# First rows asked for ahead of an expert's weights, in a kernel of two graph layers and two expert layers

## The reference, cut to what matters

```python
gate_scores = x @ Wg + bg                       # 8 experts
_, idx = jax.lax.top_k(gate_scores, K)          # K = 2 of them for each row
mask = jax.nn.one_hot(idx, E, dtype=x.dtype).sum(axis=-2)
h = jax.nn.gelu(jnp.einsum('td,edh->teh', xf, W1) + b1[None], approximate=False)
y = jnp.einsum('teh,ehd->ted', h, W2) + b2[None]
out = jnp.einsum('ted,te->td', y, mf)           # x = x + out
```

## Time and profile before

| what | value |
|---|---|
| median of 3 runs | 1220.38 us (1215.12 to 1221.03) |
| the profiled execution's own time | 1220.32 us |
| span in the profile | 1218.5 us |
| outside the span | 1.8 us |
| mean granted TensorE clock | 0.981 |
| PE busy over the span | 95% |
| DVE, ACT, POOL busy | 48%, 29%, 14% |
| PE from tile 3's turn to tile 26's (505.30 to 677.09 us) | one turn each 7.35 us where nothing is late |

### The profile page before, as it was taken

The page is one execution under the profiler, slowest core; times in us unless marked ns, Lnnn a source line. Parts: engine busy times, 40 slices in busy tenths (PEclk is TensorE's granted clock), DMA queues, the critical chain, the costliest instruction groups (busy, mean ns, idle before and its releaser), DMA issues. The chain is left out here.

```text
span 1218.5 us, 22357 instructions
## 1 busy us (share of the span) xinstructions
PE 1156.3 (95%) x7928; PEld 880.6 (72%) x7928; DVE 581.1 (48%) x1647; ACT 356.1 (29%) x769; POOL 167.0 (14%) x161
## 2 busy tenths in 40 slices
PE   5979999999999997999999869999999999999998
PEld 4658888886667885888888757655556678876675
DVE  7978888863445668411111165000034455338644
ACT  3464444442220101333333233200012201034333
POOL 4100000000000346544444400000000000001000
PEclk9989999999999998999999979999999999999999
DMA  6510000005653246465655441120046535226101
GB/s 204 179 43 12 22 12 21 22 24 170 179 153 95 93 130 192 87 113 112 147 110 91 77 135 65 61 77 28 31 118 176 157 93 178 78 70 203 50 22 41
DMA packets 134641, 117.83 MB, mean 97 GB/s; under 512 B 23334, under 2 KB 122729, under 8 KB 134560
## 3 DMA queue, kind: packets, MB, share of 16 engines
q1 hardware_dynamic: 102928, 76.88, 22.0%
q0 software_dynamic: 12368, 18.62, 7.9%
q10 hardware_dynamic: 19264, 21.24, 5.1%
HBM read 67.01 MB, written 49.29 MB: 95 GB/s over the span
## 5 line engine op out<-in xcount | busy, mean ns | idle before, releaser
L1358 PE MATMUL b_pa<-adj,l_parts 128*128 (+2 forms) x1078 | 144.9, 286 | 3.7 <-ACT ring L1286 3.7
L1358 PEld LDWEIGHTS b_pa<-adj,l_parts 128*128 128x128 f16 x1078 | 101.4, 98 | 27.2 <-issue 5.5
L1585 DVE SCALAR_TENSOR_TENSOR l_parts<-dense,scale,l_parts 128x256 f16<-128x256 f32 x48 | 23.2, 483 | 167.5 <-ACT l_parts L1576 167.4
L2767 POOL DMA_INDIRECT x<-ring,l_ids_now x56 | 87.4, 1561 | 111.5 <-DMA x<-ring,l_ids_now 60.5
L2611 PE MATMUL l_sum<-l_parts,ring 128*128 128x256 f32 x448 | 101.4, 379 | 0.4 <-issue 0.4
L615 DVE TENSOR_TENSOR ring<-it,key 128x900 f16<-128x900 f16 (+1 forms) x170 | 85.7, 546 | 31.8 <-PE dense L1342 16.0
L1552 PE MATMUL dense<-room,ring 128*128 128x512 f32 x200 | 93.9, 594 | 0.5 <-ACT ring L1533 0.5
L2611 PEld LDWEIGHTS l_sum<-l_parts,ring 128*128 128x128 f32 x448 | 83.0, 190 | 10.8 <-ACT ring L2699 0.6
L2256 PE MATMUL l_sum<-l_parts,adj 128*128 128x256 f16 x735 | 83.0, 273 | 1.3 <-DVE l_rows L1989 1.2
L2256 PE MATMUL l1b_sum<-l_parts,adj 128*128 128x256 f16 x735 | 82.9, 273 | 0.9 <-DVE l1b_rows L1989 0.9
L615 DVE TENSOR_TENSOR room<-ib,low 128x1536 f16<-128x1536 f16 x85 | 80.8, 951 | 0.0
(11 more groups left out here) (431 smaller groups left out, 1812.8 us busy)
## 6 DMA issues: line engine op xcount, KB each, us to landing
ring<-sums_and_zt SPq DMA_DIRECT2D x50, 256.0 KB, 3.2
l_parts<-in_L_ffn_W SPq DMA_DIRECT2D x16, 512.0 KB, 4.8
l_parts<-slots_in SPq DMA_DIRECT2D x28, 257.0 KB, 3.1
pre<-room ACTq DMA_DIRECT2D x34, 128.0 KB, 1.7
ring<-inv SPq DMA_DIRECT2D x50, 64.0 KB, 3.9
sums_and_zt<-room ACTq DMA_DIRECT2D x5, 640.0 KB, 3.1
adj<-xt SPq DMA_DIRECT2D x5, 640.0 KB, 4.5
adj<-x SPq DMA_DIRECT2D x5, 640.0 KB, 5.8
```

Of the source, the lines that this page charges most:

```text
L1358: ins = nc.tensor.matmul(pa[f][:, 0:size], parts[:, k, a, f * P:(f + 1) * P], adj[:, k, ds(r * BW, size)], start=k == 0 and a == 0, stop=k ...
L1585: return nc.vector.scalar_tensor_tensor(parts[:, k, 1, :], bank[:, 0:D], scale, parts[:, k, 0, :], ALU.mult, ALU.subtract)
L2767: pool.indirect_dma_start(out=g["x1"], in_=y[:, half, t, :], in_offset=None, compute_op=ALU.add, out_offset=bass.IndirectOffsetOnAxis(ap=i ...
```

## The change

The change has four edits.

1. **SP's order.** The rows of an expert's first tile are loaded before the expert's weights. The loop over an expert's tiles is moved by one: inside it `load_from_table(j + 1)` asks for tiles at+1 to the next expert's first one, and for the last expert it stops one earlier.
2. **SP's table values.** The three values of expert e+1 are read behind the weight DMAs of expert e, not ahead of its own.
3. **The last expert** counts at least two tiles (`LAST_MOST`), by one more DVE instruction on one number. The loop of edit 1 needs it. `STMAX`, the size of the tables, stays 44. With 2 tiles the last expert already has as many.
4. **POOL's last tile** is no exception any more. It waits for all the adds before it like every other tile, and POOL reads two table values less. One DVE instruction that stored a value for it is gone.

```diff
+LAST_MOST = 2
@@ Route.vector
         ch.done(nc.vector.tensor_copy(cnt[:, 1, :], cnt_i[:, 1, :]))
+        ch.done(nc.vector.tensor_scalar(cnt[:, 1, E0 - 1:E0], cnt[:, 1, E0 - 1:E0], float(LAST_MOST), None, ALU.max))
...
-        ch.mark(nc.vector.tensor_scalar(g["from"][:, 0:1], cnt[:, 2, E0 - 1:E0], -1.0, None, ALU.add))
@@ experts, sync
         later_tiles(sp, 1, load_from_table)
+        def range_on(e):
+            return (tiles_on(sp, e)[1], sp.value_load(g["tiles"][0:1, 2, ds(e, 1)], min_val=2, max_val=STMAX - (e < E0 - 1)))
+
+        following = range_on(2)
+        load_from_table(following[0])
         for e in range(2, E0):
             u = e % 2
-            _, at = tiles_on(sp, e)
-            end = sp.value_load(g["tiles"][0:1, 2, ds(e, 1)], min_val=1, max_val=STMAX)
+            at, end = following
             sp.wait_ge(s[f"w_free{u}"], e // 2)
             load_expert(sp, io, weights, e, u, s[f"w_in{u}"])
-            with sp.Fori(at, end) as j:
-                load_from_table(j)
+            if e < E0 - 1:
+                following = range_on(e + 1)
+            with sp.Fori(at, end if e < E0 - 1 else sp.snap(end - 1)) as j:
+                load_from_table(sp.snap(j + 1))
@@ experts, gpsimd
-        def add_rows(j, half, tiles_before=None):
+        def add_rows(j, half):
...
-                pool.wait_ge(s["added"], 16 * NT * (j if tiles_before is None else tiles_before))
+                pool.wait_ge(s["added"], 16 * NT * j)
...
-        pairs, odd = pool.snap(last >> 1), pool.snap(last & 1)
+        pairs, odd = pool.snap(total >> 1), pool.snap(total & 1)
...
         with pool.If(odd != 0):
             add_rows(pool.snap(pairs * 2), 0)
-            add_rows(last, 1, last_expert)
         with pool.Else():
-            add_rows(last, 0, last_expert)
+            pool.nop()
```

More of the change, by code:

```diff
@@ L59 @@
 EARLY = 4
-STMAX = -(-(2 * ROWS + sum(EARLY_ROWS) + E0 * (ST - 1)) // ST // 2) * 2
+LAST_MOST = 2
+STMAX = -(-(2 * ROWS + sum(EARLY_ROWS) + (LAST_MOST - 1) * ST + E0 * (ST - 1)) // ST // 2) * 2
 CAP = ROWS + max(EARLY_ROWS)
@@ L2774, in gpsimd @@
         total = total_on(pool)
-        last = pool.value_load(g["from"][0:1, 0:1], min_val=E0 - 1, max_val=STMAX - 1)
-        last_expert = pool.value_load(g["tiles"][0:1, 1, E0 - 1:E0], min_val=E0 - 1, max_val=STMAX - 1)
-        pairs, odd = pool.snap(last >> 1), pool.snap(last & 1)
+        pairs, odd = pool.snap(total >> 1), pool.snap(total & 1)
         with pool.Fori(1, pairs) as i:
```

## The result

The changed kernel is slower: 1222.42 us (19 runs, 1218.35 to 1224.37) against 1219.26 for the kernel before (19 runs, 1215.12 to 1222.70). The ratio is 1.0021, with a 95% interval of 1.0012 to 1.0029, so 2.6 us with 1.5 to 3.5 as bounds. A second comparison, made later with 11 and 21 runs, gave 1.0017 (1.0007 to 1.0027). The forecast was 1219.0 and a gain of 1.3 us. The time is inside the range that was given, the sign is wrong. One execution in the experiments, of the kernel with early weights, was slow (3393.9 us) and counts in no ratio.

A forecast was written before the change was run, and what follows sets the result against it. PE, busy 95% of the span, was taken as the bound. Gains of 2.2 us, less 0.6 for late weights and 0.3 for the last tile's wait, gave -1.3 us from 1220.3: 1219.0, range 1214.8 to 1224.

The forecast's parts named there:

- Gains on PE: Expert stage, turns of tiles 9, 11 and 15: rows ahead of weights save 0.92, 0.71 and 0.6, together 2.2 us.
- the 0.71 of control at tile 9: Tile 9, between turn and second product: PE's table read and branch cost 0.71 us, expected to run under queued products.
- Weights late for PE: First products after expert switches: weights issued later make PE wait 0.2 us at each of three switches, 0.6 us.
- a rival at 4.2: Late weights at tiles 9, 11, 14, 16, 19, 26, 0.7 us each: +2.3 us in all, 1222.7 us, chance 0.2.
- The estimate of the flight at expert 7: Expert 7's weights, rows issued at 671.36: landed by 680.7, needed at tile 26's first product at 680.98, margin 0.3 us.
- The rival of no change: Tile 15's wait and tile 9's control stay, 0.71 + 0.21 is paid back by weights and tail: 1220.3 us, chance 0.2.
- The wait of the last tile: POOL at tile 27, now also waiting for tile 26's adds: 0.3 us late, bounds 0 and 0.8.
- PLACE: Rival in the experiments: the lost time lies outside the expert stage, from the program's layout; no chance given.
- The rival that gave the right time (1222.7): Late weights eat the gain and more: PE waits for `w_in` 0.7 us at each of six tiles, chance 0.2.

The follow-up runs named there:

- early weights: Changed kernel with the last tile's exception back and the weights of experts 3 to 7 asked for behind the third tile's rows of the expert before: 1218.84 and 1217.40 us.
- small weights: Changed kernel with the weight matrices of experts 2 to 7 cut to one sixteenth of their columns: 1218.31 us, ratio 0.9996 to the kernel before.
- early weights with the wait: As early weights, but with the changed kernel's wait for all adds at the last tile: 1219.6 us, ratio 1.0001 to the kernel before.
- edit 4 alone: The kernel before with only the last tile's exception taken out, order of loads as before: 1219.5 us, ratio 1.0003.

## Why the prediction was wrong

**Gains on PE: right.** I had 2.2 for tiles 9, 11 and 15. The three executions of the changed kernel have 191.2, 192.0 and 191.2 against 193.8 and 193.1, a gain of 2.0 between the means. In the first one every first product from tile 1 to 11 follows by 7.35, so the 0.71 of control at tile 9 went away with the late rows: 0.92 came back, not 0.21. This agrees with the queue of 64 instructions that the Trainium skill gives TensorE ("TensorE: Matmul & The Clock Gate", architectural detail), but no run here shows the depth. Tile 15 was on time in two of three.

**Weights late for PE: too high.** I took 0.6 and had a rival at 4.2. PE waited 0.2 once in the whole stage. The estimate of the flight at expert 7, 9.3 us from the rows' issue to the last weight, was too long: rows issued at 669.62, last weight transfer at 671.8 and landed 5.3 later at 677.1, so 7.5 us, and 2 us ahead of tile 26's first product (679.23). A part of the excess is in the window of the earlier trace rows that gave 4.7 us of work for the weights: it also holds the row load issued at 671.36, which I didn't subtract. The rival of no change has a slip too: it counts three of four causes that are not the order of loads, and by my own account two of the four (0.92 of 2.7 us) are the order of loads.

**The wait of the last tile: this step failed.** I took 0.3 us with 0.8 as the bound. The tails give 3.7, 1.2 and 3.7, a mean of 2.9. Four things were wrong in it. I let POOL be on pace at expert 7. It was 2.9 us behind at tile 23 and, with expert 7's weights, 4.1 at tile 24: tile 24's first product is at 664.54, a POOL on pace follows 7.15 later (the 6.71 of the tail and 0.44 for the turn that lies between), at 671.7, and it came at 675.82. I counted a collision of weights and adds for expert 7 alone, though each of six switches has one. I had no second gap behind tile 24's adds, which cost 1.6 and 1.7 us in two of three executions. And I subtracted nothing for PE: if PE gets ahead by 2.6 us, a POOL that isn't waiting for PE falls behind by 2.6 us. From tile 0's to tile 17's adds POOL needed 124.0 us (503.49 to 627.46) where before it needed 121.5 (502.33 to 623.83). With PE's gain that makes some 5 us of lag more than before, 7.2 in all at tile 17, against 0.8 a tile of catching up. By tile 23 the tiles of expert 6 have taken back 4.3 of it, and expert 7 has two tiles.

Sum of the steps as measured: -2.0 + 0 + 2.9 = +0.9 us. The stages agree with it (means 216.8 and 215.8, +1.0). The timed difference is 2.1 to 2.6.

**What stays open.** More than 1 us lies between the two. Other kernels show as much: with small weights the stage is 2.7 us shorter than in before and the time 0.5 less (1.8 less to 0.9 more by the interval), and early weights with the wait had the longest stage, 217.3, at a ratio of 1.0001. So the tail accounts for the difference that edit 4 makes, and not for all of the time. The next stage's clock may be part of it. From PE's first transposes the granted clock took 9.9 us to return to the upper level (2.4 GHz) in the first execution of the changed kernel, and 7.9 in that of before; two windows of each, clock in the third column from the right:

```profile
713.00:715.00 2.00, 2.00 (x6) 1.57 (x6) 1.76 (x13) 1.95 (x7) 0.00 (x0) 0.57 0.33 90
715.00:717.00 2.00, 2.00 (x12) 1.76 (x10) 1.86 (x9) 1.23 (x1) 0.00 (x0) 1.00 0.67 238
```

```profile
717.00:719.00 2.00, 2.00 (x6) 1.58 (x5) 1.83 (x9) 1.45 (x3) 0.00 (x0) 0.52 0.73 257
719.00:721.00 2.00, 2.00 (x11) 1.78 (x11) 0.90 (x5) 0.17 (x1) 0.00 (x0) 1.00 0.00 0
```

The first pair is before, the second the changed kernel. But the changed kernel's other executions took 8.7 and 6.8, and the kernel with small weights 9.9 with an idle time of only 11.8. So the clock's return is worth a microsecond either way and isn't tied to the length of the idle stretch in these runs. Whether it leans against the changed kernel on average is not shown. The stage's start moved between 481.8 and 486.2 us over ten executions of kernels with the new order, three of the changed kernel itself giving 485.8, 481.8 and 482.3, so the 1.2 in the first profile is within the spread. But the three executions with the order of before all began at 484.4 to 484.6, and whether the new program moves the start on average, which is what is left of PLACE, is open.

The rival that gave the right time (1222.7) gave the wrong reason. It had PE waiting for weights at six places. What waits is POOL, at one.

## What to carry to other kernels

When an edit makes the busiest engine faster, write down the pace and the backlog of every chain that runs behind it, and carry the backlog through to the last tile. Here PE's tile is 7.35 us and POOL's 6.55, so POOL looks free, but it starts late and a collision with an expert's weights costs it up to 4 us. An exception that does nothing measurable in a kernel (edit 4 alone, 1.0003) may be what a next edit needs, so take such edits apart in the timing before they are made together. And place large transfers where the chain that they slow has tiles left to recover in.

## What the runs showed of the hardware

An indirect add of 128 rows took 3.8 us to land as the median of the stage, and up to 7.5 beside weights and rows from SP's queue. The prediction allowed 2.7 us for such a meeting, and at expert 2 it cost the small transfer 3.7. A row load of 257 KB without weights, issued 0.6 to 1.4 us behind the second of two adds, went with 1.2 to 1.9 us more until the next tile's, and with nothing where it was issued 2.1 us behind. The return of TensorE's clock behind an idle stretch of 11 to 15 us came 6.8 to 9.9 us after its first work, without order by the length of the idle stretch, which moves a single execution by about 1 us.
